# Own rows of a relation table chosen by eight predicated copies, in place of two mask products and a sum over the kinds

## The reference

```
# layer 0: message passing
msg = relu((x[src] * edge_weight) @ W_msg + b_msg)
agg = segment_sum(msg, dst)
x1  = layernorm(x + relu(agg @ W_out + b_out))
# layers 1 and 2: relational, 8 kinds of edge
xt  = einsum('nd,rde->rne', x, W)           # a table of 8 rows per node
agg = segment_sum(xt[kind, src], dst)
x   = relu(agg + x @ SW + b)
# after the second: layernorm(x1 + x)
```

## Time and profile before

| | us |
|---|---|
| median of 3 runs | 7073.51 |
| lowest, highest | 7067.35, 7080.22 |
| the profiled execution's own time | 7068.35 |
| its span, first to last instruction | 7066.6 |
| granted TensorE clock, mean | 0.631 |

### The profile page before, as it was taken

How to read it: one execution, slowest core, us unless ns; L and a number is a source line. 1 busy time by engine, 2 the same in 40 slices (tenths; PEclk the granted TensorE clock), 3 DMA queues, 4 the chain that set the end, 5 groups by cost and what they waited for, 6 DMA issues and landing times.

```text
span 7066.6 us, 46612 instructions
## 1 busy us (share of the span) xinstructions
PE 2678.6 (38%) x11862; PEld 2091.1 (30%) x11862; DVE 2579.4 (37%) x4881; ACT 1033.7 (15%) x2878; POOL 4511.1 (64%) x4794
## 2 busy tenths in 40 slices
PE   6233434433444434444444444443222322222223
PEld 5223323332333323333222332322222222222223
DVE  4777666466545523333233233322111111111112
ACT  2233333333333300000000000000000000000000
POOL 5666666666666456666666666665666666666665
PEclk8666666666666656666666666665555555555556
DMA  5122222322222212222222222221121111111111
GB/s 154 46 81 74 73 70 69 84 72 79 78 75 79 71 56 70 70 70 70 67 70 70 68 70 70 70 67 56 51 53 51 52 53 52 52 52 52 51 51 50
DMA packets 279550, 471.55 MB, mean 67 GB/s; under 512 B 110125, under 2 KB 169385, under 8 KB 279270
## 3 DMA queue, kind: packets, MB, share of 16 engines
q0 software_dynamic: 152672, 312.98, 17.0%
q1 hardware_dynamic: 125446, 155.09, 6.5%
q10 hardware_dynamic: 1152, 0.39, 0.0%
HBM read 346.02 MB, written 122.09 MB: 66 GB/s over the span
## 4 chain that ended last, share of the span: by engine, by line
another core or an unknown queue 31%; issue 31%; PE 17%; DVE 14%; ACT 4%; SPq 1%; DMA 1%; DVEq 1%; POOL 0%; ACTq 0%; POOLq 0%
PE bank L869 10%; PE bank L1123 5%; ACT rows L697 2%; DVE onehot L816 2%; DVE place L1185 2%; DVE picked L1174 1%; DVE rows L833 1%; DVE work L816 1%; DVE tab L1195 1%; ACT rows L715 1%; DVE bank L1541 1%; DVE work L1542 1%; DVEq L852 1%; DVE bank L1534 1%
## 5 line engine op out<-in xcount | busy, mean ns | idle before, releaser
L749 POOL DMA_INDIRECT rows<-rel_table,rel_index x3152 | 2973.8, 943 | 1641.6 <-issue 936.8
L749 POOL DMA_INDIRECT rows<-msg_table,msg_index x1555 | 1469.3, 945 | 851.3 <-issue 456.4
L869 PE MATMUL bank<-work,rows 128*128 128x128 f32 x6304 | 1200.4, 338 | 1235.4 <-issue 1209.9
L857 DVE TENSOR_TENSOR agg<-agg,bank 128x128 f32 x597 | 170.4, 285 | 3735.6 <-remote 3277.4
L869 PEld LDWEIGHTS bank<-work,rows 128*128 128x128 f32 x6304 | 1092.9, 250 | 1381.9 <-issue 1355.9
L869 PE MATMUL bank<-onehot,rows 128*128 128x128 f32 x3238 | 610.8, 361 | 912.7 <-ACT rows L715 443.0
L869 PEld LDWEIGHTS bank<-onehot,rows 128*128 128x128 f32 x3238 | 566.0, 266 | 990.3 <-ACT rows L715 471.6
L1123 PE MATMUL bank<-wr,feat 128*128 128x512 f32 x784 | 598.0, 906 | 656.9 <-issue 464.3
L697 ACT ACTIVATE rows<-rows,weight 128x128 f32<-128x128 f32 x1555 | 493.5, 388 | 984.2 <-DVE onehot L816 528.2
L816 DVE TENSOR_TENSOR work<-bank,place 128x1024 f32<-128x1024 f32 x394 | 476.8, 1211 | 7.3 <-ACT agg L1034 3.8
L1123 PEld LDWEIGHTS bank<-wr,feat 128*128 128x128 f32 x784 | 205.0, 290 | 858.1 <-issue 654.0
(11 more groups left out here) (145 smaller groups left out, 1630.1 us busy)
## 6 DMA issues: line engine op xcount, KB each, us to landing
rel_table<-tab SPq DMA_DIRECT2D x196, 512.0 KB
rows<-rel_table,rel_index POOLq DMA_INDIRECT x3152
rows<-msg_table,msg_index POOLq DMA_INDIRECT x1555
x_dram<-normed SPq DMA_DIRECT2D x98, 64.0 KB
xin<-x_dram SPq DMA_DIRECT2D x98, 64.0 KB
xin<-in_x_dram SPq DMA_DIRECT2D x97, 64.0 KB
out_dram<-normed SPq DMA_DIRECT2D x97, 64.0 KB
tab<-in_x_dram SPq DMA_DIRECT2D x24, 256.0 KB
```

Of the source, the lines that this page charges most:

```text
L749: nc.gpsimd.indirect_dma_start(rows[:, u, t, :], None, table, bass.IndirectOffsetOnAxis(ap=table_index[:, g, t:t + 1], axis=0)).then_inc(e ...
L857: nc.vector.tensor_tensor(out=window, in0=window, in1=sum_of(layer, st), op=ALU.add).then_inc(sems.added, 1)
L869: ins = nc.tensor.matmul(total, tile, hot[:, t, :], start=t == 0, stop=t == most - 1)
```

## The change

The two products and the sum give way to eight predicated copies. For each kind r, DVE copies the 128 columns of kind r from `ps_tab` straight to the own-row slot, in the partitions where column r of `chosen` isn't zero. Each copy waits for the one before, the fifth also for ACT's copy of the second bank. The wait for a free slot stands ahead of the first copy. A block counts 9 in `pick` (mask and eight copies) where it counted 4, and `table_free` waits for all nine of the block before, where it waited for three of four. `dve_own_row` and its call are gone.

```diff
@@ table_free
             if trim:
-                need(eng, sems.pick, PICKS * st.n - 1)
+                need(eng, sems.pick, PICKS * st.n)
@@
-        PICKS = 4
+        PICKS = 1 + R
@@ dve_pick
             v.wait_ge(sems.pick, done + 1)
-            for h in range(2):
-                if h:
+            need(v, sems.joined, st.n - OWN_ROWS + 1)
+            for r in range(R):
+                if r == R // 2:
                     v.wait_ge(sems.taba, st.n + 1)
-                part = slice(h * R // 2, (h + 1) * R // 2)
-                v.tensor_tensor(
-                    out=picked[:, h * H:(h + 1) * H].rearrange("p (r e) -> p r e", r=R // 2),
-                    in0=ps_tab[h][:, :].rearrange("p (r e) -> p r e", r=R // 2),
-                    in1=chosen[:, k, part].unsqueeze(2).to_broadcast([P, R // 2, D]),
-                    op=ALU.mult).then_inc(sems.pick, 1)
-
-        def dve_own_row(sems, st):
-
-
-            need(nc.vector, sems.joined, st.n - OWN_ROWS + 1)
-            nc.vector.wait_ge(sems.pick, PICKS * st.n + 3)
-            nc.vector.tensor_reduce(out=own_row_of(st.b),
-                                    in_=picked[:, :].rearrange("p (r e) -> p e r", r=R), axis=AX,
-                                    op=ALU.add).then_inc(sems.pick, 1)
+                v.wait_ge(sems.pick, done + (1 + r))
+                v.copy_predicated(
+                    own_row_of(st.b),
+                    chosen[:, k, r:r + 1].bitcast(I32).to_broadcast([P, D]),
+                    ps_tab[r * 2 // R][:, r * D % H:r * D % H + D]).then_inc(sems.pick, 1)
@@ dve_nodes, at its end
-            st = stage(PRODUCTS[layer] + 1) if trim and layer < 2 else None
-            if st is not None:
-                dve_own_row(sems, st)
```

## The result

The changed kernel takes 7090.98 us (median of 8 runs, 7087.94 to 7106.05), the kernel before 7071.59 in the same comparison: a ratio of 1.0031, 95% interval 1.0022 to 1.0040. It is slower by 19 us: inside the wide range, outside the likeliest case's 7050 to 7084 us, and of the other sign. The profiled execution took 7088.28 us, its span is 7086.5.

The account below looks back on a forecast made before the run. Gathers run during 6801 of 7066.6 us, their pace set by POOL's issue and its waits for row buffers released by PE's group matmuls. Terms -9 + 4.1 - 1.1 = -6 us gave 7067 us, range 7028 to 7100.

Parts of the forecast that it names:

- the wide range: Whole kernel: 7028 to 7100 us, reaching to both outcomes of the stands and the quarter cases.
- the likeliest case: Whole kernel: the forecast itself, 7067 us with its own range 7050 to 7084, chance 0.58.
- The body of the first layer: First layer's gather stretch: one-hot 0.4 us sooner counts in about a quarter of 89 blocks, -9 us; bounds -36 and +52.
- What hides it in the stretches: Gather stretches: second layer gains 0, first layer -9 us; later normalization covered by PE's 4.31 us before the next group.
- The second rival: Normalization pushed back, where PE's idle time is under 1.39 us: about 7200 us in all blocks, 7107 in a quarter; chance 0.10.
- The third rival: POOL's stands fall differently in the first layer, 27 us either way, 7040 or 7094 us; chance 0.14.
- The 3.0 us that a block's picks took without a wait: First layer, each block: old products and sum take 3.33 us, 3.0 without the 0.24-us wait for ScalarE; new copies 2.60.
- The end of the first layer: After the first layer's gathers run out: copies lie on the path, 2.60 us where 1.2 lay; sum +4.1 us.
- The second layer's body and the third: Second layer's gathers hide the picks, 0 us with bounds 0 and -9.5; third layer has no pick, 0.
- The end of the second layer: Three blocks gain 0.59 us each, last-but-one's feature copy is released 0.65 us later; sum -1.1 us.
- The copy's price: Each 128-column predicated copy: 0.30 us, chained at 0.336; bounds 0.30 and 0.48, eight taking 2.3 to 3.6 us.

Follow-up runs that it names:

- the second pair: Kernel before and changed kernel, both unchanged, profiled again at the 7070 level; the changed kernel took 7094.14 us against 7070.46, ratio 1.0030.
- its turn moved: Kernel before with the last of four layout turns (PE transposes edge-table piece, VectorE unpacks) one step later, 75 for 74; 1.0001 at 6088 level.
- The old sum early: Kernel before with the strided sum directly behind the two products; 1.0022 at the 6088 level, 1.0027 at the 7070 level.
- the copies late: Changed kernel with the eight copies where the sum stood, behind normalization and statistics; against the kernel before 0.9999 at the 6088 level, 1.0005 at the 7070 level.

## Why the prediction was wrong

*The body of the first layer, forecast -9 us, measured +18.8 and, in the second pair, +16.7.* This is the step that failed, "What hides it in the stretches": the later normalization was put at nothing, and the stands of POOL at a turn had no term.

The later normalization was costed at nothing: "1.39 fits in 4.3, and the one-hot comes sooner". It was 1.50 us later, and the cover was where the forecast saw it, in every block. The idle time between a block's small matmuls and the next group is never under 3.09 us in the two profiles before (94 blocks, median 4.31), and its median in the changed kernel is 2.5. By the forecast's own rule, that lateness decides where this idle time is under 1.39 us, it should have decided nowhere. It was moved instead: PE waits less behind the small matmuls (its waits for weighed rows fell from 443.0 to 355.3 us, in the second pair from 471.5 to 351.6) and more ahead of them (for own sums and normalized rows together from 172.2 to 294.3, and from 217.4 to 289.4). And the loss came all the same: groups 60 to 156 pay 8.8 and 5.9 us, of which single stands of POOL, 4.1 us more ahead of group 70 and 5.7 more ahead of group 86, are a half and nearly all. With the copies behind the normalization the kernel's loss is gone. What was wrong is thus the step from "covered at PE's next wait" to "costs nothing"; by which path the lateness reaches POOL stays open. The second rival had the direction, with a fraction of a quarter of the blocks and a chance of 0.10, but its condition, idle time under 1.39 us, was met in none.

The other part, 10.6 and 11.9 us, had no term: the turn's handshake. The first profile before shows the turn served within 0.5 us and right after a stand of POOL; 25 us after a stand it was served after 8.7 in the second profile, yet without a loss at 156 to 160. A hint was there in the kernel before: "remote" waits of 676 us on POOL's side. I read the stands as a matter of cycles of two, four or five groups and priced their shift at 27 us either way. The third rival's price was the right size, its place was not: their number hardly changed (97 of over 1 us in the first stretch in both profiles, 101 and 98 in the second pair), their sum did, by 15.6 and 15.2 us.

The 3.0 us that a block's picks took without a wait is 3.33 - 0.24 = 3.09 by the rows that the forecast names; 3.0 comes out with the 1.20 of the earlier trace rows for the products. The gain of 0.4 us a block that made the -9 is not seen at the 7070 level. At the 6088 level the same stretch is 1966.6 us in the kernel before and with its turn moved, 1970.0 and 1969.8 in the two other kernels with the old operations in the first layer, and 1964.3 to 1965.8 in four with the new. That is -1 to -6 us, the sign and nearly the size of the forecast, though kernels with the same first layer differ there by 3.4 us.

*The end of the first layer, forecast +4.1.* At the 6088 level the wait of POOL is 54.6 and 54.5 us with the old operations in the first layer (51.3 with the turn moved) and 60.3, 59.2, 59.2 and 59.2 with the new: +5. The old sum early adds 11.0, six blocks of 1.88; the copies late add 1.0. The mechanism and size are right at this level. At the 7070 level it was +1.3 and +10.9 in the two pairs, on both sides of the forecast and too far apart to confirm it; the rows after, of both profiles:

```profile
2539.03 0.95 POOL L749 DMA_INDIRECT rows<-rel_table,rel_index  x1 [91.23 <-DMA rel_table<-tab]
```

```profile
2550.01 0.94 POOL L749 DMA_INDIRECT rows<-rel_table,rel_index  x1 [98.72 <-DMA rel_table<-tab]
```

*The second layer's body and the third, forecast 0:* +0.2 and -1.2. Right, and the cover was sound: 576.11 us busy of 2252.1.

*The end of the second layer, forecast -1.1:* 31.2 to 32.5 us at the 7070 level (33.3 to 33.2 in the second pair), 21.4 to 22.4 at the 6088 level, but 21.6 in the run with the new copies in the second layer only. The forecast gain didn't come; that the copies' release of ScalarE's feature copy is why is likely, not shown. The row after the earlier trace rows:

```profile
4815.11 0.31 ACT L1082 ACTIVATE feat<-agg 128x128 f32<-128x128 f32 x1 [1.66 <-DVE place L1175]
```

0.84 became 1.66 us, 0.82 where 0.65 was forecast.

*The copy's price, forecast 0.30 at a pitch of 0.336:* 0.300 at 0.344; the first starts 0.35 us behind the comparison's start, where the first product started 0.25 behind it. The estimate from the Trainium skill's table (page "VectorE: DVE Perf Modes", section "The TRN2 errata") was 0.258; here the row is nearer. The forecast says that the trace agrees with both rules that it draws from that page. What it quotes, 1.88 us against 0.69, bears on the reduction; on the fixed part of a small instruction bears its fit of the earlier trace rows, 162 ns.

Taken together, the sum without the first layer's body would have been -6 + 9 = +3 us, and at the 6088 level the kernel measures +4. The forecast's arithmetic comes near that level; the profile in hand was of the other.

*What stays open.* Why "remote" signals are late at the 7070 level isn't shown: the runs show when they are late, not what carries them, nor what set the level. Nor is it shown by which path the later normalization reaches POOL. Single stands of 5 to 14 us that differ between two profiles of one kernel (groups 70 and 86), or of kernels alike up to there (118), leave the gradual part known to some 3 us at best. Whether the old kernel's turn can be moved to where VectorE follows late was tried at the 6088 level only, where it always follows at once.

## What to carry to other kernels

Look for waits that end by nothing in the profile, and ask of each one-time handshake, not only of each loop's, what the engines did just before it: here VectorE followed late where POOL had issued for 9 us or more. A gap behind a later step, even one that is there in every block, doesn't make the later step free: it also moves what comes ahead of the gap, and the view of waits gives both totals. Instructions saved on an engine whose time is hidden are worth nothing, but their order still counts: the same copies moved behind the normalization cost nothing that the times can tell, and in front of it 0.3%.

## What the runs showed of the hardware

One program with the same instruction times ran at two levels 16% apart, 6088 and 7071 us, and one chip showed both, at 6088 and 7116. At the slower one the waits of POOL that no record explains sum to 676 us, those of VectorE to 3459; at the faster there are none. VectorE followed PE's four transposes by 0.0 to 2.4 us where POOL had stood within 5.6 us before, and by 2.3 to 21.7 us, most of it idle, where POOL had issued gathers at their pitch of 1.25 us for 9 us or more.

A predicated copy of 128x128 from PSUM took 298 to 306 ns in 1568 cases, chained at 0.344 us. The strided sum of 1024 elements to 128 took 1.88 us, so eight chained copies of 128 (2.71 us) cost less than the products and the sum together (1.29 and 1.88 us), and more than either alone.
